# TensorE waits for single banks and chunks in layer 1's keys and scores and in layer 0's output projection; f1's sums open without products of zeros

## The reference

```python
x = layernorm(x + L0_attn(x))     # linear attention: phi = elu + 1
x = layernorm(x + L0_xattn(x))    # 4 experts ("x0") picked by token id
x = layernorm(x + L0_ffn(x))      # 8 experts ("f0"), gated weights
x = layernorm(x + L1_attn(x))     # attention in groups of 32 positions
x = layernorm(x + L1_xattn(x))    # attention to a context ("x1")
x = layernorm(x + L1_ffn(x))      # top 2 of 8 experts and a shared one ("f1")

# L0_attn, after its heads are joined:       out @ o_w.T + o_b
# L1_attn: q, k, v = x @ W.T + b, half of the heads rolled by 16;
#   scores = einsum('bhgqd,bhgkd->bhgqk', qg, kg) / 4, masked, softmax, times v
# L1_ffn:
act = silu(gu[..., :F]) * gu[..., F:]
y = einsum('tef,te,ehf->th', act, combine, down) + sact @ shared_down.T
```

## Time and profile before

| | |
|---|---|
| median of 3 runs | 436.26 us (435.32 to 437.35) |
| the profiled execution | 435.11 us, span 433.3 us |
| PE busy | 415.2 us, 96% of the span |
| DVE, ACT, POOL busy | 264.2, 241.6, 276.7 us |
| PE on the chain that ended last | 79% |
| TensorE's mean granted clock | 0.994 |

### The profile page before, as it was taken

The page is one execution under the profiler, slowest core; times in us unless marked ns, Lnnn a source line. Parts: engine busy times, 40 slices in busy tenths (PEclk is TensorE's granted clock), DMA queues, the critical chain, the costliest instruction groups (busy, mean ns, idle before and its releaser), DMA issues.

```text
span 433.3 us, 9358 instructions
## 1 busy us (share of the span) xinstructions
PE 415.2 (96%) x3649; PEld 362.3 (84%) x3649; DVE 264.2 (61%) x637; ACT 241.6 (56%) x423; POOL 276.7 (64%) x237
## 2 busy tenths in 40 slices
PE   8999999999999999899999999899979999999993
PEld 6788999988889888688888898688868989888882
DVE  4778657758536338956664588555654676445463
ACT  4937653764484765352743867463636757453533
POOL 1744454564798576665876458457768287787863
PEclk9999999999999999999999999999989999999999
DMA  8644000021233313132222103212532332555402
GB/s 257 190 147 136 12 2 0 2 73 51 73 95 121 110 41 122 30 119 95 82 81 76 38 2 109 73 64 63 156 118 63 122 103 69 159 160 147 138 31 98
DMA packets 19623, 39.29 MB, mean 91 GB/s; under 512 B 2763, under 2 KB 7371, under 8 KB 19580
## 3 DMA queue, kind: packets, MB, share of 16 engines
q1 hardware_dynamic: 19004, 38.17, 28.3%
q10 hardware_dynamic: 576, 0.53, 0.4%
HBM read 37.08 MB, written 1.08 MB: 88 GB/s over the span
## 4 chain that ended last, share of the span: by engine, by line
PE 79%; DVE 11%; ACT 3%; issue 3%; DMA 2%; POOL 1%; SPq 1%; DVEq 0%; POOLq 0%; ACTq 0%
PE bank L487 14%; PE bank L490 13%; PE bank L488 13%; PE bank L756 8%; PE bank L758 8%; PE bank L757 8%; PE bank L832 2%; DMA pk_raw<-w_attn_dram 2%; PE bank L775 2%; DVE hraw L1616 1%; DVE sil L1600 1%; PE bank L820 1%; PE bank L510 1%; PE bank L806 1%; PE bank L804 1%
## 5 line engine op out<-in xcount | busy, mean ns | idle before, releaser
L1298 POOL TENSOR_TENSOR h_lo<-hraw,h_hi 128x512 fp32r<-128x512 f32 x76 | 100.7, 1328 | 74.7 <-ACT h_hi L1088 74.7
L487 PE MATMUL bank<-xT_hi,pk_hi 128*128 128x512 f32 x256 | 102.9, 402 | 1.1 <-DVE hraw L1616 1.1
L488 PE MATMUL bank<-xT_hi,pk_lo 128*128 128x512 f32 x256 | 101.0, 395 | 0.0
L1088 ACT ACTIVATE h_hi<-hraw 128x512 fp32r<-128x512 f32 x76 | 47.8, 629 | 75.2 <-DVE hraw L1616 73.2
L1616 DVE TENSOR_TENSOR hraw<-bank,sil 128x512 f32<-128x512 f32 x76 | 52.4, 689 | 52.1 <-ACT sil L1076 24.6
L490 PE MATMUL bank<-xT_lo,pk_hi 128*128 128x512 f32 x256 | 80.5, 395 | 0.0
L756 PE MATMUL bank<-pk_hi,h_hi 128*128 128x256 f32 x272 | 78.5, 288 | 1.2 <-POOL h_lo L1298 1.0
L757 PE MATMUL bank<-pk_lo,h_hi 128*128 128x256 f32 x272 | 77.5, 285 | 0.0
L758 PE MATMUL bank<-pk_hi,h_lo 128*128 128x256 f32 x272 | 77.5, 285 | 0.0
L1304 POOL TENSOR_TENSOR pk_lo<-pk_raw,pk_hi 128x512 fp32r<-128x512 f32 (+1 forms) x44 | 75.1, 1707 | 2.7 <-ACT pk_hi L1106 2.5
L1309 POOL TENSOR_TENSOR pk_lo<-pk_raw,pk_hi 128x256 fp32r<-128x256 f32 (+1 forms) x44 | 43.8, 995 | 24.3 <-ACT pk_hi L1117 24.3
(11 more groups left out here) (257 smaller groups left out, 732.2 us busy)
## 6 DMA issues: line engine op xcount, KB each, us to landing
pk_raw<-pk_f_dram SPq DMA_DIRECT2D x28, 384.0 KB, 3.3
pk_raw<-pk_f_dram SPq DMA_DIRECT2D x16, 512.0 KB, 3.6
pk_raw<-pk_f_dram SPq DMA_DIRECT2D x16, 256.0 KB, 3.0
kv_buf<-pk_x_dram SPq DMA_DIRECT2D x4, 512.0 KB, 3.5
x_tok<-x_rows_dram SPq DMA_DIRECT2D x1, 1024.0 KB, 9.9
pk_raw<-pk_x_dram SPq DMA_DIRECT2D x4, 256.0 KB, 6.0
brow<-cw_dram SPq DMA_DIRECT2D x4, 256.0 KB, 3.2
cw_late<-cw_dram SPq DMA_DIRECT2D x4, 256.0 KB, 4.5
```

Of the source, the lines that this page charges most:

```text
L487: pe.matmul(o, w(kc)[0], x(kc)[0], start=kc == 0, stop=False)
L488: pe.matmul(o, w(kc)[1], x(kc)[0], start=False, stop=False)
L1088: A(h_hi[:, row, at * 512:(at + 1) * 512], hraw[:, s % 2, :], ACT.Copy).then_inc(sems["hid_hi"], 1)
L1298: pool.tensor_tensor(h_lo[:, row, q], hraw[:, s % 2, :], h_hi[:, row, q].bitcast(F32), ALU.subtract).then_inc(sems["hid_lo"], 1)
```

## The change

`a0_project` goes through the chunks outside and the tiles inside, and waits for each chunk by itself. Two tiles of one bank are then open at once, so only the bank's first product starts anew (`start`), and the other tile's first product comes to columns that this start has cleared. The keys wait for the queries' move out of bank 6 before c = 0 and out of bank 7 before c = 1. The first scores wait for the third tile's values before r = 0 and for the fourth's before r = 1. `open_sums` becomes `sums_free`, which only waits; the first down product of each bank in f1's first chunk starts the sum. All other down products take their start by the bank too, with the same number of products in the same order.

```diff
-                pe.wait_ge(sems["a0_aT_lo"], KC * (h + 1))
-                for t in range(HT):
-                    o = q_bank(h, t // 2)[:, (t % 2) * D:(t % 2 + 1) * D]
-                    for kc in range(KC):
+                for kc in range(KC):
+                    pe.wait_ge(sems["a0_aT_lo"], KC * h + kc + 1)
+                    wh, wl = wa(kc, 3 * D, 4 * D)
+                    for t in range(HT):
+                        o = q_bank(h, t // 2)[:, (t % 2) * D:(t % 2 + 1) * D]
...
-                        pe.matmul(o, ah, wh, start=kc == 0, stop=False)
+                        pe.matmul(o, ah, wh, start=kc == 0 and t % 2 == 0, stop=False, skip_group_check=True)
...
-            def open_sums(h):
+            def sums_free(h):
...
-                for j in range(2):
-                    pe.matmul(bank[4 + j][:, :], zero_r[:, 0:P], zero_r[:, :], start=True, stop=False,
-                              skip_group_check=True)
...
+                fresh = closed or m % N1 == 0
...
-                        pe.matmul(o, hh, vh, start=closed and kc == 0, stop=False, skip_group_check=not closed)
+                        first = fresh and kc == 0 and t % 2 == 0
+                        pe.matmul(o, hh, vh, start=first, stop=False, skip_group_check=True)
...
                 for c in range(KC):
                     if h and j == 0 and c:
                         pe.wait_ge(sems["cwT_done"], 1)
+                    elif j:
+                        pe.wait_ge(sems["a1_q"], KC * h + c + 1)
...
                 for r in range(2):
+                    if T0 is not None:
+                        pe.wait_ge(sems["a1_v"], T0 + 3 + r)
...
                 elif i == 4:
-                    pe.wait_ge(sems["a1_q"], KC * (h + 1))
                     a1_project(h, 1)
...
                 elif i == 7:
-                    pe.wait_ge(sems["a1_v"], T0 + HT)
-                    a1_scores(2 * h)
+                    a1_scores(2 * h, T0)
```

More of the change, by code:

```diff
@@ L640, in a0_project @@
                     pe.wait_ge(sems["wa_lo_done"], 2)
-                pe.wait_ge(sems["a0_aT_lo"], KC * (h + 1))
-                for t in range(HT):
-                    o = q_bank(h, t // 2)[:, (t % 2) * D:(t % 2 + 1) * D]
-                    for kc in range(KC):
+                for kc in range(KC):
[3 more added lines that the diff above has]
+                        o = q_bank(h, t // 2)[:, (t % 2) * D:(t % 2 + 1) * D]
                         a = kc * 512 + t * P
                         ah, al = aT_hi[h][:, a:a + P], aT_lo[h][:, a:a + P]
-                        wh, wl = wa(kc, 3 * D, 4 * D)
-                        pe.matmul(o, ah, wh, start=kc == 0, stop=False)
[L649 to L652, removed]
+                        pe.matmul(o, ah, wh, start=kc == 0 and t % 2 == 0, stop=False, skip_group_check=True)
+                        pe.matmul(o, ah, wl, start=False, stop=False, skip_group_check=True)
+                        m = pe.matmul(o, al, wh, start=False, stop=kc == KC - 1 and t % 2 == 1, skip_group_check=True)
+                        if kc == KC - 1 and t % 2:
+                            m.then_inc(sems["a0_o_ps"], 1)
             def first(i, h):
@@ L741, in down @@
                     if m % N1 == 0:
-                        open_sums(m // N1)
+                        sums_free(m // N1)
                     pe.wait_ge(sems["d_lo"], 2 * E0 + m + 1)
@@ L755, in down @@
                         vh, vl = wh[:, kc * D:(kc + 1) * D], wl[:, kc * D:(kc + 1) * D]
-                        pe.matmul(o, hh, vh, start=closed and kc == 0, stop=False, skip_group_check=not closed)
-                        pe.matmul(o, hh, vl, start=False, stop=False, skip_group_check=not closed)
-                        m_ = pe.matmul(o, hl, vh, start=False, stop=closed and kc == chunks - 1,
-                                       skip_group_check=not closed)
+                        first = fresh and kc == 0 and t % 2 == 0
+                        pe.matmul(o, hh, vh, start=first, stop=False, skip_group_check=True)
+                        pe.matmul(o, hh, vl, start=False, stop=False, skip_group_check=True)
+                        m_ = pe.matmul(o, hl, vh, start=False, stop=closed and t % 2 == 1 and kc == chunks - 1,
+                                       skip_group_check=True)
                     if t % 2 and closed:
@@ L807, in a1_value, with a1_scores @@
                 m.then_inc(sems["a1_v_ps"], 1)
-            def a1_scores(b):
+            def a1_scores(b, T0=None):
                 h = b // 2
                 for r in range(2):
+                    if T0 is not None:
+                        pe.wait_ge(sems["a1_v"], T0 + 3 + r)
                     rows = slice(QH * HD * r, QH * HD * (r + 1))
```

## The result

| | before | changed |
|---|---|---|
| median (range, runs) | 435.32 us (432.36 to 437.86, 21) | 432.52 us (430.04 to 434.23, 21) |
| profiled execution | 435.11 us, span 433.3 | 431.72 us, span 429.8 |
| PE busy, mean granted clock | 415.2 us, 0.994 | 414.1 us, 0.997 |

The ratio is 0.9922, 95% interval 0.9904 to 0.9939: 3.4 us faster (2.7 to 4.2), where I had forecast 0.9916 and 3.65 us. The two medians by themselves lie 2.80 us apart.

A forecast was written before the change was run, and what follows sets the result against it. PE, busy 96% of the span, was taken as the bound. Gains 0.65 + 0.66 + 1.02 + 0.12 + 0.74 + 0.46 = 3.65 us took 435.11 to 431.46, scaled (0.9916) to 432.6 us; range 429.6 to 435.2.

The forecast's parts named there:

- A: Layer 0's output projection, half 0: PE needs only the first low part from DVE before going on; gain 0.65 us.
- B: Layer 1's keys, half 0: PE starts after DVE's first bank move, not both; gain 0.66 us, a 0.3 us wait stays.
- C: Layer 1's keys, half 1: first move is done before PE ends the queries, so the stop goes; gain 1.02 us.
- D: Opening of half 0's sums (d24): two products worth 0.46 us go, but PE then waits for ACT's keys; gain 0.12 us.
- added waits: Six places get a wait, and d24 and d38 wait for three counters; cost taken as 0, bounds 0 and 0.5 us.
- sharpest sign: At a1.5, a new stop of 0.3 us before the values, ended by ACT L1154, where there was none.
- E: First scores of layer 1, half 1: r = 0 needs only the third tile's values, not the fourth's; gain 0.74 us.
- F: Opening of half 1's sums (d38): two products go and the gain reaches the tail; 0.46 us.
- R1: Time saved early is lost at 163 to 184 us where another engine is late; 434.2 us, chance 0.20.
- R2: PE's longest unexplained stop in a1_values and its slow stretch go, 2.9 us more won; 429.7 us, chance 0.11.
- R3: Stops and slow stretch come twice, in half 0 too, cancelling the gain; 436.3 us or slower, chance 0.05.
- R4: A wait for one bank is in effect for both, leaving 0.92 us of gain; 435.3 us, chance 0.06.

The follow-up runs named there:

- padded by 29: Changed kernel with three of nine warm-up products replaced by 32 products of 64 columns, 29 more ahead of everything; 433.20 us, ratio to before 0.9963.
- scores alone: Kernel before, with only layer 1's first scores call waiting for single tiles of values; 435.88 us, ratio 1.0016.
- the padding and the split: Changed kernel, one warm-up product replaced by 33 tiny ones, layer 1's first two value products each waiting for their own bank of keys; 428.59 us, ratio to before 0.9857.
- projection alone: Kernel before, with only layer 0's output projection going chunk-outer, one wait for each chunk of aT; 435.53 us, ratio 0.9987.
- openings alone: Kernel before, with only the two pairs of zero products that open f1's sums removed; 435.62 us, ratio 0.9997.
- the second trace: The changed kernel run again, unaltered; 432.06 us, ratio to before 0.9916.
- before, padded: Kernel before, with one of nine warm-up products replaced by 33 products of 32x32x32, 32 more ahead of everything; 433.10 us, ratio 0.9935.
- changed, padded: Changed kernel with one of nine warm-up products replaced by 33 products of 32x32x32, 32 more ahead of everything; 428.83 us, ratio to before 0.9861.
- (keys): Kernel before, with only layer 1's key products waiting per bank, in both halves; 434.78 us, ratio 0.9981.
- (split): Changed kernel, layer 1's first value product waiting only for VectorE's move of keys, the second for ScalarE's; 432.99 us, ratio to before 0.9935.

## Why the prediction was right, and where its parts were off

**A, projection: 0.65 forecast, 0.62 measured.** The time from h_lo's start to the first hraw is 15.77 to 15.79 us in the five traces without the edit and 15.18 to 15.19 in the nine with it. That the landmark at 44 us came 0.52 earlier and not 0.62 is the start: h_lo began at 28.48 and not 28.38, and it ranged from 27.54 to 29.62 over the traces, the one padded by 29 left out.

**B, keys of half 0: 0.66 forecast, 0.64 measured.** The wait of 0.3 us that I left is there as 0.18 in the row.

**C, keys of half 1: 1.02 forecast, 1.13 measured, and D, opening of d24: 0.12 forecast, 0.00 measured.** The sum of the two was right (1.14, 1.13) because one term was missing from both, with opposite signs. A product that PE had to wait for starts its successor late, by 0.11 us with 512 columns: after the stop at 279.26 the next starts at 279.60, 0.34 later, and without one 0.23 later (276.86, 277.09). C removes such a stop wholly and wins 0.11 more; D makes a new one and loses 0.11 up to the scores (6.50 for 6.39). I had seen the longer record (0.36 against 0.28) and used it for the added waits alone. The sharpest sign, a stop before the values ended by ACT's kx, is there: 0.21 us (I had written 0.3).

**E, scores: 0.74 forecast, 0.51 measured.** This is the term that was mis-sized, by two parts. The time from the first value product to the scores fell by 0.65 (6.39 to 5.74 with the scores alone) and not by 0.74, since the first score starts 0.21 us behind the last value product and not 0.12. And the 64 products took 1.66 us and not 1.49. I had looked only at whether the fourth tile is there in time. It is, by less than 0.1 us: in the kernel with the padding and the split it lay at 288.97 + 0.49 = 289.46, and PE, at its usual pace, would come to the second half at 288.87 + 0.68 = 289.55. The record is 1.73 us there as well, as in all nine traces with the edit, and 1.56 in the five without. But it isn't the wait as such. The scores of half 0 get the same two waits. Their fourth tile was moved 0.79 us before they start, and their record is 1.56 us in the nine traces with the edit as in the five without. The changed kernel, half 0 and half 1:

```profile
197.11 1.56 PE L823 MATMUL bank<-kx,q_buf 64*32 64x128 f32 x64
...
288.68 1.73 PE L823 MATMUL bank<-kx,q_buf 64*32 64x128 f32 x64
288.79 0.49 DVE L1712 TENSOR_TENSOR kv_buf<-bank,bv 128x128 f32<-128x128 f32 x2 [0.93 <-PE bank L807]
```

In half 1 the first 0.08 of the 0.17 is lost at the 21st product (289.25), twelve ahead of the second wait and just before the tile is there (289.28). That looks as if PE's list is read some products ahead, so that a counter must be there earlier than its product. No run moved the tile against the wait, so this reading isn't shown.

**F, opening of d38: 0.46 forecast, 0.44 measured.** No engine became late behind it.

**The added waits: 0 forecast.** Right for A, for the keys and for the scores of half 0, wrong by 0.17 in the scores of half 1, where the counter came less than 0.1 us ahead.

**The rivals.** R1 said that A would be lost at 163 to 184 us. The projection alone keeps it. POOL's part and DVE's bk_four moved together by 0.50 us, so DVE's 2.25 us beside POOL are in the chain but not fixed in time. R2 had the right place and the wrong reason: the stops did change, yet not because 3 us had passed. They follow the list, as the rows against it said: with the two zero products of d24 gone, the place went from 123 of the first block to 125, and from 85 of the fourth to 87 (projection and openings alone). Only which of the places stops, and for how long, differs. The slow stretch I had priced at 1.7 us from the mean clock. Its products of 256 columns start 0.21 us apart and not 0.12, fifteen of them from 322.18 to 325.38, so it costs 15 x 0.09 = 1.4. In the changed kernel's trace half 0 has no stop (0.32 less), and half 1 has 0.92 more of stops and no slow stretch (1.4 less); 0.4 of this is gone again by 332 us. A net 0.27 is left in the two columns, and the second trace has -0.22: chance. R3 didn't come, though single traces (the projection alone: -2.28 and -1.12) show that stops of its size are common. R4 is refuted by B, C and E in every trace.

**What this means for the forecast.** The ledger's 3.34 us lies in the measured 2.7 to 4.2, so the stops added nothing on average that this measurement can tell (-0.6 to 0.9). The traces say the same: half 1's column of stops has a mean of -0.8 us over the four traces with before's list, and the same over the four without d24's zeros that are neither padded nor cut. That my 3.65 came within 0.3 of the 3.4 is finer than the interval, and in part luck, since C was too low by what D was too high. Starts in the changed trace are earlier by 0.51, 1.15, 3.01 and 3.52 us at 168, 197, 300 and 410 us, where I had written 0.65, 1.3, 3.2 and 3.65 for nearly these places. The stops made the profiled spans differ by up to 5 us from one kernel to the next, and my range of 5.6 us had much of its width from them.

## What to carry to other kernels

Price an edit by the stretch that it touches and compare landmarks, not ends: parts of half a microsecond repeated within 0.1 us while whole times scattered by 5. A stop costs its idle time and 0.1 us more. A split wait inside a burst of tiny products was free where its counter came 0.8 us ahead and cost 0.17 us where it came less than 0.1 ahead, so ask by how much a wait is met, not only whether. When a burst of tiny products stops for "issue", shift the burst against the instruction list with a few cheap products ahead: here that was worth 3 us, nearly as much as all the edits together.

## What the runs showed of the hardware that I had not expected

TensorE's instructions come in lots. Its stops in a1_values lie 127 or 128 products apart in the list: after 125 of a block 3 are left, 12 products follow, and 112 of the next make 127. They moved by 29 when 29 products were put ahead, and by 32 for 32. In the trace of before, padded, half 1's third block shows a stop of 0.25 us after 65 products; 97 - 32 = 65. A product is a weight load and a matmul, so 128 products are 256 instructions, less where semaphore instructions stand between them. Counted with these, in the records of all fourteen traces, the 32 stops of a1_values stand at the 193rd or 194th of 256 without exception. The page of the changed kernel shows a queue of the kind "instruction" (packets, MB, share):

```profile
q8 instruction: 29, 0.48, 0.4%
```

In the packed trace each of the 29 packets has 16384 bytes; 29 x 128 is 3712, and PE has 3645 products. The Trainium skill (Runtime: NRT & Kernel Launch, Instruction fetch mechanics) says that the list is refilled in blocks of 16 KiB, 256 instructions, while the block before is executed, at a cost that is "mostly hidden". The traces agree with the size. They differ on the cost: in a burst the longest stop was 2.25 to 2.61 us in seven of the eight traces with whole, unshifted blocks of half 1, and in the eighth there were two of 1.06 and 1.23.

The packets show what ends these stops. The page doesn't list them one by one, but the packed trace has the time of each. In all 32 stops PE goes on 1.2 to 1.5 us behind the end of a packet of q8. The lot that PE needs within half 1's first block (us; q1 is the queue of the weights):

| kernel | q1's transfer | q8's packet | PE stops | PE goes on |
|---|---|---|---|---|
| changed | 301.55 to 303.33 | 303.26 to 304.64 | 303.36 | 305.93 |
| projection alone | 306.40 to 308.16 | 308.15 to 309.51 | 308.19 | 310.79 |
| before | 304.57 to 306.38 | 303.92 to 304.84 | no stop | |
| changed, padded | 301.21 to 302.98 | 294.32 to 295.59 | no stop | |

In each of the seven traces with the long stop the packet begins in the last 0.12 us of a transfer on q1; in before it came ahead of the transfer. So the packet seems to stand in line behind the weights, though no run took them away, and what let it pass ahead in before is open. Its own length doesn't depend on them: the median of all packets is 0.99 us beside next to no transfers as well as beside busy ones.

From the first product of a lot to the first of the next can thus be 4 to 5 us, while a burst uses a lot up in 1.3. The changed kernel begins one two products before the first block, at 301.80; the packet of the next lot begins 1.46 us later and takes 1.37, and PE goes on 1.30 behind it, at 305.93. The next lot is needed at 310.21 and work goes on at 310.85, 4.9 us later. In the changed, padded kernel 34 products ahead of the block are in the same lot, which begins 4.2 us ahead of it, and there was no stop.

The clock fell with some of these stops and not with others: to 0.50 for 6.8 us in the traces with stops of 2.61 (projection), 2.25 (keys), 2.59 (openings) and 2.34 us (split), for 3.4 us after 2.39 (scores), and not after 2.57 and 2.32 in the two traces of the changed kernel. What decides is open. In the five traces with a list longer at its start the clock was full from 300 to 332 us.
